# One Mamba block and gated FFN on one core: dt_proj's bias as a 17th row of the product, softplus's first two steps by whole PSUM banks

## What is computed

```
xz = h @ in_proj_w.T;  u, z = split(xz)              # d_inner 512
uc = silu(causal conv of u, 4 taps)
dt, B, C = split(uc @ x_proj_w.T, [16, 32])          # dt has 16 columns, B and C 16 each
dt = softplus(dt @ dt_proj_w.T + dt_proj_b)          # 16 -> 512, with a bias per channel
h_t = exp(dt * A) * h_(t-1) + dt * B_t * uc          # 16 states for each of 512 channels
y = (h_t . C_t + uc * D) * silu(z);  out = y @ out_proj_w.T + x
FFN: silu(x w1) * (x w2), gelu(. h1), gelu(. h2), . w3
```

## Time and profile before

| | |
|---|---|
| median of 3 runs | 1458.85 us (1458.41 to 1460.64) |
| the profiled execution | 1458.7 us, of which the span of its instructions is 1456.9 us |
| granted TensorE clock, mean | 0.946 |
| busy, share of the span | PE 88%, PEld 80%, DVE 90%, ACT 82%, POOL 78% |
| chain that ended last, by engine | PE 36%, DVE 22%, ACT 20%, POOL 10%, issue 9%, DMA 2% |

### The profile page before, as it was taken

One profiled execution on the slowest core, in us unless ns is written; L12 is line 12 of the kernel. 1 busy time (PEld: TensorE's weight loads), 2 busy tenths in 40 slices (PEclk: granted clock), 3 DMA queues, 4 the chain that ended last, 5 costly groups with the idle time before them and its releaser, 6 DMA issues.

```text
span 1456.9 us, 27022 instructions
## 1 busy us (share of the span) xinstructions
PE 1280.5 (88%) x9264; PEld 1171.0 (80%) x9264; DVE 1308.3 (90%) x1993; ACT 1197.1 (82%) x2605; POOL 1135.3 (78%) x1351
## 2 busy tenths in 40 slices
PE   6556789899998999899998989999899989898897
PEld 4244588798988989798897889888898979888797
DVE  6999998999999998999999899999999899998842
ACT  6555688989898888989888898989888898987753
POOL 4746778888888888888888888888898888788620
PEclk8576899999999989999999999999999999999999
DMA  7400111110111111110111111011111110010100
GB/s 276 156 17 30 43 26 38 39 39 24 46 31 42 35 39 38 38 35 27 45 32 46 38 39 39 24 43 34 39 39 39 38 38 31 24 47 24 31 4 17
DMA packets 39168, 63.21 MB, mean 43 GB/s; under 512 B 5248, under 2 KB 19456, under 8 KB 38928
## 3 DMA queue, kind: packets, MB, share of 16 engines
q10 hardware_dynamic: 18944, 33.83, 7.4%
q1 hardware_dynamic: 19984, 26.02, 5.6%
HBM read 55.38 MB, written 4.46 MB: 41 GB/s over the span
## 4 chain that ended last, share of the span: by engine, by line
PE 36%; DVE 22%; ACT 20%; POOL 10%; issue 9%; DMA 2%; SPq 0%; ACTq 0%; DVEq 0%; POOLq 0%
DVE S L1730 8%; PE fP L784 7%; PE fP L785 7%; DVE acc L1744 6%; PE sT L808 5%; POOL S L592 5%; POOL Glo L662 4%; ACT dA L1310 4%; PE fP L772 3%; PE hP L772 3%; ACT Rw L1471 2%; ACT Rw L1438 2%; ACT Ghi L1479 2%; PE hP L951 2%; PE fP L983 2%
## 5 line engine op out<-in xcount | busy, mean ns | idle before, releaser
L592 POOL TENSOR_TENSOR S<-X,Bs 128x1024 f32<-128x1024 f32 x255 | 609.6, 2391 | 131.0 <-PE sT L808 99.5
L1730 DVE TENSOR_TENSOR_SCAN S<-dA,S 128x512 f32<-128x512 f32 x512 | 620.1, 1211 | 45.7 <-POOL S L595 22.8
L1310 ACT ACTIVATE dA<-delta,A 128x255 f32<-128x255 f32 x1024 | 444.6, 469 | 172.5 <-DVE S L1730 171.8
L808 PE MATMUL sT<-ident,S 128*128 128x128 f32 x2048 | 323.7, 285 | 93.3 <-DVE acc L1744 88.6
L784 PE MATMUL fP<-Ghi,w_h 128*128 128x256 f32 x1512 | 380.5, 291 | 0.4 <-ACT Rw L1497 0.4
L785 PE MATMUL fP<-Glo,w_h 128*128 128x256 f32 x1512 | 363.7, 279 | 0.0
L1744 DVE SCALAR_TENSOR_TENSOR acc<-sT,CT,acc 128x512 f32<-128x512 f32 x480 | 347.0, 726 | 13.0 <-PE sT L808 13.0
L808 PEld LDWEIGHTS sT<-ident,S 128*128 128x128 f32 x2048 | 244.2, 146 | 136.0 <-DVE S L1730 83.4
L784 PEld LDWEIGHTS fP<-Ghi,w_h 128*128 128x128 f32 x1512 | 284.8, 188 | 6.8 <-ACT Rw L1497 5.1
L785 PEld LDWEIGHTS fP<-Glo,w_h 128*128 128x128 f32 x1512 | 284.9, 188 | 0.0
L662 POOL TENSOR_TENSOR Glo<-Rw,Ghi 128x1024 fp32r<-128x1024 f32 x86 | 203.9, 2370 | 28.2 <-ACT Ghi L1509 19.4
(11 more groups left out here) (280 smaller groups left out, 2329.2 us busy)
## 6 DMA issues: line engine op xcount, KB each, us to landing
Bs<-b_rows ACTq DMA_DIRECT2D x128, 256.0 KB, 3.2
xh<-in_x SPq DMA_DIRECT2D x16, 256.0 KB, 2.9
xt<-in_x SPq DMA_DIRECT2D x16, 256.0 KB, 3.1
out<-x SPq DMA_DIRECT2D x15, 256.0 KB, 2.2
Rw<-in_w SPq DMA_DIRECT2D x4, 512.0 KB, 4.3
Rw<-in_h SPq DMA_DIRECT2D x4, 512.0 KB, 5.9
delta<-in_h SPq DMA_DIRECT2D x3, 512.0 KB, 3.8
X<-in_h SPq DMA_DIRECT2D x3, 512.0 KB, 7.1
```

What stands on the lines that cost most here:

```text
L592: pool.tensor_tensor(s[:, :, :], X[par][:, :, :], row[:, None, :].broadcast_to([P, DT, T]), ALU.mult).then_inc(scan_pool.sem, 1)
L808: mm = pe.transpose(sT[t][:, d * P:(d + 1) * P], S[slot(third, n)][:, d, t * P:(t + 1) * P], ident[:, :])
L1310: a = act.activation(dA[half][:, i, 1:], delta[par][:, d, 1:], ACT.Exp, scale=A[:, d * N + n:d * N + n + 1])
L1730: a = dve.tensor_tensor_scan(pair, dA[half][:, :, :].rearrange("p d t -> p (d t)"), pair, 0.0, ALU.mult, ALU.add)
```

## The change

Chunks 1 to 15 get the bias from the product. w_dt has a 17th row, which holds dt_proj_b for all 512 channels, and the product's other operand is xdbl[64:81], whose row 80 must be one. Row 80 of the product of x_proj is zero; ACT's copy to xdbl becomes an Identity activation with a bias operand that is one on partition 80 and zero elsewhere: a column of the identity matrix. B, C and dt have other rows and stay as they are. The relu and the absolute value then need no bias, and each takes a whole bank of 128 x 512 in one instruction: 4 instructions for a chunk where there were 8. Chunk 0's own head stays as before and uses the first 16 rows.

The 17th row is loaded by one more transfer on SP's queue, before the load of stage 12. It reads the bias out of `cols`, where neighbouring channels are a row of `cols` apart, so its 512 values are 512 separate pieces of 4 bytes; they all go to one partition. PE waits for it once, in chunk 1's head.

```diff
-        w_dt = sb("w_dt", [AT_DT + R, DI])[AT_DT:AT_DT + R, :]
+        w_dt = sb("w_dt", [AT_DT + R + 1, DI])[AT_DT:AT_DT + R + 1, :]
+        dtx_and_one = xdbl[AT_DT:AT_DT + R + 1, :]
+        one_row = ident[0:XC, AT_DT + R:AT_DT + R + 1]
+        dt_bias_in = sem("dt_bias_in")
-            sp.dma_start(w_dt, dt_proj).then_inc(small_in, 16)
+            sp.dma_start(w_dt[0:R, :], dt_proj).then_inc(small_in, 16)
                 if s == 12:
+                    sp.dma_start(w_dt[R:R + 1, :].rearrange("o (d p) -> o d p", p=P),
+                                 cols[:, col_at["dt_b"]:col_at["dt_b"] + DT].rearrange("p d -> d p")[None, :, :],
+                                 allow_slow_non_contiguous=True)\
+                      .then_inc(dt_bias_in, 16)
                     pe.wait_ge(head_act.sem, head_act.at(h, "dtx"))
+                    if h == 1:
+                        pe.wait_ge(dt_bias_in, 16)
-                            mm = pe.matmul(hP[q][:, d, :], w_dt[:, m * P:(m + 1) * P], dtx, start=True, stop=True)
+                            mm = pe.matmul(hP[q][:, d, :], w_dt[:, m * P:(m + 1) * P], dtx_and_one,
+                                           start=True, stop=True)
-                    act.copy(xdbl[:, :], hP[1][0:XC, 0, :]).then_inc(head_act.sem, 1)
+                    act.activation(xdbl[:, :], hP[1][0:XC, 0, :], ACT.Identity, bias=one_row).then_inc(head_act.sem, 1)
-                    for i in range(2):
-                        d = 2 * q + i
-                        act.activation(delta[hp][:, d, :], hP[q][:, i, :], ACT.Relu, bias=c_("dt_b", d))
-                        a = act.activation(hP[q][:, i, :], hP[q][:, i, :], ACT.Abs, bias=c_("dt_b", d))
-                    a.then_inc(head_act.sem, 1)
+                    act.activation(delta[hp][:, 2 * q:2 * q + 2, :], hP[q][:, :, :], ACT.Relu)
+                    act.activation(hP[q][:, :, :], hP[q][:, :, :], ACT.Abs).then_inc(head_act.sem, 1)
```

More of the change, by code:

```diff
@@ L1120, in _ @@
                     m = 2 * q + d
-                    mm = pe.matmul(hP[q][:, d, :], w_dt[:, m * P:(m + 1) * P], dtx, start=True, stop=True)
+                    mm = pe.matmul(hP[q][:, d, :], w_dt[0:R, m * P:(m + 1) * P], dtx, start=True, stop=True)
                 mm.then_inc(first_pe.sem, 1)
```

## The result

The changed kernel takes 1446.4 us (1444.9 to 1447.7, 6 runs) where the kernel before takes 1458.7 in the same session: a ratio of 0.9913, 95% interval 0.9902 to 0.9924. Forecast were 1448.9 and a range of 1446.0 to 1455.5. The profiled execution took 1446.2 us, its span 1444.4.

The account below looks back on a forecast made before the run. No engine bounds the kernel alone; around softplus ACT leads DVE. Fourteen heads at 0.75 (10.5) plus 0.4 for chunk 1's, less 1.0 for the transfer, take 9.9 us off: median 1448.9 us, range 1446.0 to 1455.5.

Parts of the forecast that it names:

- I take 1.0 us of delay for Bs: Chunk 0's start: the 4-byte transfer delays the B load that POOL waits for by 1.0 us, bounds 0 and 8.
- ACT's stretch: ACT before softplus's exp: four wide instructions replace eight, first relu to exp 2.11 us instead of 3.01, a gain of 0.90.
- DVE takes only its own wait: DVE's X after softplus's exp: faster ACT work moves DVE by at most its wait, about 0.8 us a chunk.
- What is late next: PE's row from POOL's Glo to the gather of state 15: DVE moves by 0.6 us there rather than 0.82.
- rival A: Whole chunk: PE's row moves as well, so the full 0.82 us passes, 11.4 us off, 1447.4; chance 0.11.
- The seven steps: PE's row of turns, 784.56 to 801.34: waits of 0.47 us go, seven turns in 16.3 us instead of 16.78.
- the gap of 0.15 behind the turn near 820: PE at tile L784: its 0.15 us of waiting for ACT's bank copy goes too.
- Per chunk: Heads of chunks 2 to 15: 0.60 + 0.15 = 0.75 us each, 10.5 us over 14.
- Chunk 1's head: Softplus in chunk 0's body: DVE's wait for the exp is shorter there, so the gain is 0.4 us.
- Rival B: PE's row: its waits are replaced by the next in line, 0.30 us a chunk, 1455.2; chance 0.16 for 1452 to 1456.
- rival C: ACT's wide relu and absolute value cost twice the small form, no change; chance 0.09 including a B with dear transfer.
- The xdbl copy with its column: ACT's copy to xdbl: the bias column adds 0.12 us, covered by a wait for DVE, cost on the path 0.

Follow-up runs that it names:

- The run with the moved sum: The changed kernel with POOL's end-step sum moved from half-step 21 to 23, behind the Glo that PE waits for: 1442.6 us, ratio 0.9890, period 82.31.

## Where the prediction was off, and where it was right

- **The step that failed** is "I take 1.0 us of delay for Bs", the one term of the sum whose value was picked between wide bounds (0 and 8) rather than read from a row. The transfer costs 0 as far as can be measured: added to the kernel before, it changed the time by a factor of 0.9997 (0.9988 to 1.0005, so at most 0.7 us), and moving or dropping it changed nothing. B's load was not held back at all, POOL's first product started at 35.77 us instead of 37.93, where the prediction looked for 38 to 40. A piece took 9 ns of an engine, not 16, and the loads that the transfer does push back are SP's own, not B's, which ACT issues. With this term at 0 and 0.78 a chunk the sum is 10.9 + 0.4 = 11.3 us, 1447.4.
- ACT's stretch: forecast 3.01 to 2.11 us, measured 2.09. Right; taking the exp's row as the price of the wide forms was the right choice.
- DVE takes only its own wait, about 0.8: right. X follows its gather with no idle in the changed kernel, and taking another microsecond off ACT gives nothing.
- What is late next: PE's row of tiles behind POOL's Glo, as forecast, and not rival A's even shift. The seven steps closed from 16.78 to 16.28 (forecast 16.3), the gap of 0.15 behind the turn near 820 went, and DVE waits 0.18 us for PE at the gather of state 15. The run with the moved sum shows that this row was the bound: starting it earlier gives 0.12 us a chunk with the change and nothing without. That the measured time, 1446.4, is 1.0 below rival A's 1447.4 is therefore no sign for A.
- Per chunk: forecast 0.75, measured 0.78, which makes 10.9 us instead of 10.5. The closeness is in part luck. From X to the gather of state 15 are 17.26 us before and 17.55 in the changed kernel (most chunks, by the starts on the timeline), so the gather gained 0.83 - 0.29 = 0.54 where the forecast had 0.60; what comes behind it gained 0.24 where it had 0.15. No run separates what the further 0.09 is.
- Chunk 1's head: the wait there was 0.45, near the 0.4 taken, but by luck. At the 0.82 of the other rows 14 waits would have left only 0.1; in the trace 13 waits are 0.82 or 0.83 and another one is 0.41. Whether the 0.4 reached the total can't be told from the scatter of the first X.
- Rival B (the waits in PE's row are replaced) is out by the period and the turns, rival C by the 0.58 us of the relu and absolute value.
- The xdbl copy with its column: it lasts 0.45 us instead of 0.36 and, as forecast, costs nothing (the kernel with the plain copy has the same period). The row count of the product: nothing.
- The rest, from 11.3 to the 12.2 of the first session, is within what sessions differ by (12.2, 12.4 and 10.6). All 17 timed executions of the changed kernel have a median of 1446.7 (1444.8 to 1449.9), all 51 of the kernel before beside them 1458.7 (1455.8 to 1461.6): 12.0 off. Single executions of one kernel lie within 6 us of each other, and the first X came between 114.4 and 117.6 us in the changed kernel's three profiles. The lapse of the clock in the profile above is one such thing. What of the last 0.7 us is chance is not settled; no run separates it.

The same term stood in the range: its fast edge, 1446.0, was set from rival A, which had 0.5 us for the transfer in it, and the measured 1446.4 lies only just inside.

## What to carry to other kernels

Before pricing a faster stretch, look for the wait that it ends, then for the next engine's own row up to the place where both meet: the smaller of the two gains, plus the small waits inside the second row that fall away because their cause moved, is what passes. When a chain goes through all engines once per chunk, the test of who is bound is cheap: shorten the suspected one further by leaving work out, and start the other earlier; each gave nothing while the other led. No row showed that B's load, on another engine's queue, must stand behind the new transfer, and its cost was 0: here a zero with a wide bound would have been the better value than one in the middle.

## What the runs showed of the hardware

- A [128, 1] bias operand costs ScalarE 0.08 us per instruction in a dense row (0.36 against 0.28 between starts, 128 x 256), and 256 more columns 0.21 (0.28 to 0.49, the spacing in the changed kernel). This agrees in kind with the Trainium skill ("ScalarE: Activation LUTs", section "What ACT_TABLE_LOAD costs"), which gives 0.093 us for each pointer operand and 0.833 ns an element, 0.213 us for 256.
- The 512 pieces of 4 bytes take SP 0.84 us to issue and 9 ns of an engine each, but the load issued right behind them took 2.6 to 3.0 us to issue in the eight profiles with the early transfer where it took 0.43 without, and 2.35 us for the load of x with the late one. Nothing was late by it here: ACT's first cast of the load into X starts with no idle time ahead of it in all thirteen profiles.
- TensorE's granted clock fell to about its lower level within a long busy stretch (0.53 from 530 us, PE busy 4.5 us of 5), and the chunk took 1.3 us more. One such lapse is nearly half of what a comparison of this kernel can tell (2.9 us). Shorter lapses (0.66 over 5 us) cost the kernel before nothing, as they came out of DVE's wait for the exp, and go with distances 0.3 to 0.5 us longer in the changed kernel, where PE's row leads.
